# Odd rows of a finished chunk stored from ScalarE's transfer queue instead of SyncE's, in a two-layer convolution kernel

## What is computed

```python
# layer 0: depthwise 3x3, then three 64x64 channel mixes
dw  = conv(x, depthwise_weights, groups=64, padding=1)
att = einsum('cd,bdhw->bchw', softmax(attention_weights), dw)
pw  = einsum('kc,bchw->bkhw', pointwise_weights, att)
out = einsum('cd,bdhw->bchw', softmax(global_attention_weight), pw)
# layer 1: 3x3 convolution of signs with signed weights
xb  = sign(x);  bw = sign(clip(w, -1, 1)) * mean(abs(clip(w, -1, 1)))
out = conv(xb, bw, padding=1)
# both together; _gn is a group norm with 32 groups of 2 channels
x = x + layer0(_gn(x), ...)
x = x + layer1(_gn(x), w)
```

## Time and profile before

| | |
|---|---|
| median of three runs | 1862.25 us |
| the three runs | 1861.27, 1862.25, 1868.79 us |
| profiled execution, its own time | 1867.16 us |
| its span in the trace | 1865.3 us |
| mean granted TensorE clock | 0.998 |
| PE busy | 1767.8 us, 95% |
| DVE busy | 1603.3 us, 86% |
| ACT busy | 1333.6 us, 71% |
| POOL busy | 580.4 us, 31% |
| transfers | 271.39 MB, mean 145 GB/s |

### The profile page before, as it was taken

The page is one execution under the profiler, slowest core; times in us unless marked ns, Lnnn a source line. Parts: engine busy times, 40 slices in busy tenths (PEclk is TensorE's granted clock), DMA queues, the critical chain, the costliest instruction groups (busy, mean ns, idle before and its releaser), DMA issues.

```text
span 1865.3 us, 76406 instructions
## 1 busy us (share of the span) xinstructions
PE 1767.8 (95%) x33132; PEld 1535.2 (82%) x33132; DVE 1603.3 (86%) x2605; ACT 1333.6 (71%) x1460; POOL 580.4 (31%) x353
## 2 busy tenths in 40 slices
PE   0299999999999999999999999999999999999997
PEld 0299987799888887889988888779988888889996
DVE  5878889888998889888898888988899888877776
ACT  2277777677777776777777777777777777677774
POOL 1133333233233332333333333323333333333331
PEclk9999999999999999999999999999999999999999
DMA  9725665556555665656655666556655655433234
GB/s 283 194 81 159 158 152 143 153 153 154 148 150 163 154 153 143 158 149 155 158 138 160 159 156 154 142 159 153 153 146 155 164 151 153 103 82 75 74 77 103
DMA packets 278624, 271.39 MB, mean 145 GB/s; under 512 B 16112, under 2 KB 278320, under 8 KB 278464
## 3 DMA queue, kind: packets, MB, share of 16 engines
q1 hardware_dynamic: 269568, 260.11, 54.1%
q10 hardware_dynamic: 8448, 8.39, 1.6%
q0 software_dynamic: 448, 0.73, 0.2%
HBM read 134.95 MB, written 134.22 MB: 144 GB/s over the span
## 4 chain that ended last, share of the span: by engine, by line
PE 85%; DVE 8%; DMA 3%; issue 2%; ACT 2%; ACTq 0%; SPq 0%; DVEq 0%
PE psA L511 73%; PE psB L511 12%; DMA ring<-in_x 3%; DVE bnt L734 2%; DVE ring L944 1%; ACT xh L388 1%; DVE ring L910 1%; DVE psL L940 1%; DVE pk L921 1%; DVE aggr L848 1%; DVE xc L902 1%; ACT xn L384 0%; ACT xc L357 0%; DVE sums L750 0%; DVE ring L949 0%
## 5 line engine op out<-in xcount | busy, mean ns | idle before, releaser
L511 PE MATMUL psA<-xh,W 64*64 64x512 f16 x17912 | 1552.4, 373 | 15.6 <-DVE xh L969 6.6
L511 PEld LDWEIGHTS psA<-xh,W 64*64 64x64 f16 x17912 | 1080.9, 106 | 137.6 <-issue 71.3
L511 PE MATMUL psA<-xl,W 64*64 64x512 f16 x9216 | 989.9, 376 | 0.7 <-issue 0.6
L307 POOL TENSOR_TENSOR xl<-xc,xn 128x1024 f16<-128x1024 f32 (+1 forms) x320 | 570.8, 1794 | 1203.5 <-ACT xn L384 1187.9
L511 PEld LDWEIGHTS psA<-xl,W 64*64 64x64 f16 x9216 | 593.5, 107 | 38.1 <-issue 2.3
L511 PE MATMUL psB<-pk,W 64*64 64x512 f16 (+1 forms) x4944 | 604.9, 362 | 2.3 <-DVE pk L921 1.9
L388 ACT ACTIVATE xh<-xc 64x1024 f16<-64x1024 f32 (+2 forms) x622 | 574.5, 941 | 9.2
L384 ACT ACTIVATE xn<-xc 128x1024 f16<-128x1024 f32 (+2 forms) x262 | 270.8, 1036 | 278.1 <-PE psA L511 199.5
L910 DVE SCALAR_TENSOR_TENSOR ring<-psA,columns,ring 128x1024 f32<-128x1024 f32 x256 | 328.4, 1283 | 142.1 <-PE psA L511 141.9
L511 PEld LDWEIGHTS psB<-pk,W 64*64 64x64 f16 x4944 | 301.0, 106 | 64.8 <-issue 51.3
L734 DVE BATCH_NORM_STATS2 bnt<-ring 128x6 f32<-128x512 f32 x512 | 325.7, 681 | 30.7 <-DMA ring<-in_x 30.1
(11 more groups left out here) (104 smaller groups left out, 109.6 us busy)
## 6 DMA issues: line engine op xcount, KB each, us to landing
out_y<-ring SPq DMA_DIRECT2D x512, 256.0 KB, 3.3
ring<-in_x SPq DMA_DIRECT2D x448, 256.0 KB, 4.0
ring<-in_x SPq DMA_DIRECT2D x16, 512.0 KB, 16.8
ring<-in_x ACTq DMA_DIRECT2D x16, 512.0 KB, 16.5
pk<-in_w1T POOLq DMA_DIRECT2D x2, 144.0 KB, 7.2
ring<-in_w1n POOLq DMA_DIRECT2D x2, 144.0 KB, 8.0
grp<-in_same_group POOLq DMA_DIRECT2D x1, 64.0 KB, 7.3
ring<-in_dw POOLq DMA_DIRECT2D x2, 2.2 KB, 6.7
```

The source lines that it names most:

```text
L307: ins = nc.gpsimd.tensor_tensor(xl[:, slot:slot + rows, 1:W + 1], xc[:, j:j + rows], xn[:, k:k + rows, 1:W + 1], ALU.subtract)
L511: mm = pe.matmul(bank[out0:out0 + C, c0:c1], weights[src0:src0 + C, :], src[src0:src0 + C, slot:slot + rows, width[0]:width[0] + width[1]] ...
```

## The change

`store_chunk` on SyncE issues only the transfer of the even rows. A new `store_odd` on ScalarE issues the transfer of the odd rows of the same chunk, from ScalarE's own queue. In step t it stands behind the rounding of chunk t-3 and stores chunk t-4; in the tail it stands behind the signs, and then behind each of the last three roundings. It has the waits that the store on SyncE has: `y_rdy`, and the completion of the store of chunk g-2. The two transfers count up the same semaphore as before, so what the loads wait for is unchanged: both halves.

```diff
                 at = place(img, i)
-                for r in range(2):
-                    sp.dma_start(ov[img, r, :, i * G:i * G + G, :],
-                                 ring[64 * r:64 * r + 64, at:at + CE]).then_inc(stored[g % 2], 16)
+
+                sp.dma_start(ov[img, 0, :, i * G:i * G + G, :], ring[0:64, at:at + CE]).then_inc(stored[g % 2], 16)
...
+            def store_odd(g):
+                img, i = divmod(g, NC)
+                act.wait_ge(y_rdy, g + 1)
+                if g >= 2:
+
+                    act.wait_ge(stored[g % 2], 32 * (g // 2))
+                at = place(img, i)
+                nc.scalar.dma_start(ov[img, 1, :, i * G:i * G + G, :],
+                                    ring[64:128, at:at + CE]).then_inc(stored[g % 2], 16)
+
...
                 if t >= LAG:
                     round_of(t - LAG)
+                if t > LAG:
+                    store_odd(t - LAG - 1)
...
             for g in range(ALL + 1 - LAG, ALL):
                 signs_of(g)
+            store_odd(ALL - LAG - 1)
             for g in range(ALL - LAG, ALL):
                 round_of(g)
+                store_odd(g)
```

## The result

| | before | changed |
|---|---|---|
| median of 20 runs | 1866.47 us | 1869.14 us |
| lowest and highest | 1861.27, 1870.17 | 1866.87, 1870.94 |
| profiled execution (span) | 1867.16 (1865.3) | 1869.56 (1867.7) |

The ratio of the changed kernel to the one before is 1.0016, with a 95% interval from 1.0009 to 1.0023: 1.7 to 4.3 us slower. That is a real difference, though inside the 0.5% that the prediction called the same. Two of the three runs known at the time of the prediction (median 1862.25) were the two fastest of the 20; the median of all lies 4.2 us higher.

The account below looks back on a forecast made before the run. TensorE, busy 95%, was taken to bound the kernel. Steady part 0, loads 0 and tail +1.0 us gave 1868.2 us from the profiled execution, 1863.3 us moved to the median of the runs; range 1859.0 to 1870 us.

Parts of the forecast that it names:

- Steady part: ScalarE's steady steps: the new issue runs beside the rounding, its waits are already over, and `xn` is not delayed; 0 us.
- The 1.675 us: Longest issue of a store before the change, put behind the steady rounding as upper bound; still 0 on TensorE.
- the third rival: ScalarE's queue holds up issues in steady steps; beyond 2.3 us each tenth costs 26 us, 2.4 us gives 1889 us; chance 0.02.
- Loads: SyncE's loads behind the stores: in the typical step they go out at the same time as before; taken as 0 us.
- the room of 2.97 us: Steady step: time between a load's landing at 916.85 and VectorE's statistics at 919.82, more than the 2 us of possible lateness.
- The tail: Last three roundings delayed by issues ahead of them, less a saving at the last store: +1.0 us, ends -0.5 and +4.5.
- 0.3 + 0.62 + 0.62 = 1.54 us: Tail: delays of the last three roundings, each with a transfer issued ahead of it on ScalarE.
- The 0.52 us: End of the tail: saving from issuing the last store's two halves side by side, subtracted from the roundings' delays.
- saves 0.65, less what issuing at once costs: Last store: side-by-side issue saves 0.65 us, less 0.13 us because simultaneous issues take longer.
- The first: Steady loads: earlier loads remove VectorE's 13 waits; at most -6.7 us, giving 1856.6 us; chance 0.08.
- The second: Steady loads: stores land later and loads come late, deciding from about 3 us of added delay; 3.1 us gives 1884 us; chance 0.03.
- The fourth: Issues on the two queues exclude each other, so the odd half leaves as before; tail +1.5, 1863.8 us; chance 0.05.

Follow-up runs that it names:

- e4: Changed kernel with both halves of every store issued from ScalarE behind the rounding, also in the tail; SyncE only loads: ratio to before 0.9991, median 1864.68 us.
- e6: Changed kernel with the odd half of chunk t-5 stored behind the signs of step t, ahead of the rounding; tail order kept: ratio to before 0.9983, 1862.91 us.
- e10: Both halves of chunk t-5 issued from ScalarE behind the signs of step t, in the tail behind the roundings: ratio to before 1.0098, 1886.6 us.
- e5: Changed kernel with the odd half of chunk t-5 instead of t-4 stored behind the rounding of step t: ratio to before 1.3761, 2568.1 us.
- e1: Changed kernel with the last four chunks stored wholly by SyncE, as before the change: ratio to before 1.0005, median 1868.19 us.
- e3: Changed kernel with each odd store of the tail put behind the rounding, as in the steady part: ratio to before 1.0005.
- e7: The changed kernel again, the same program with an empty line: ratio to before 1.0018.
- e2: Kernel before with only the last four odd halves stored from ScalarE, each ahead of a rounding: ratio to before 1.0009.
- e9: Changed kernel with the odd half of chunk t-5 behind the signs of step t, in the tail behind the rounding: ratio to before 0.9964, 1860.27 us.

## Why the prediction was right, point by point

**Steady part, 0 us.** Right. The issue lies beside the rounding, the waits are over when it comes, `xn` starts when TensorE lets it. e4 shows that double the issues fit. The 1.675 us that I took as the bound of an issue and the 3.49 us of the third rival never came near: 0.652 us was the longest.

**Loads, 0 us.** Right within what the runs tell. Loads go out as early as before, and the room of 2.97 us is real: a delay of about 2.9 us (e6: issued at 907.74, where the rounding of the step before ran at 904.74) is borne, 3.6 us (e10) costs 1%, 6.8 us (e5) costs 700 us. VectorE's waits for loads were 11.5 to 14.4 us in the four profiles with the odd half behind the rounding (changed, e1, e3, e7) and 6.7 and 9.1 with the old store (before, e2). If that reaches the end at all, it is within the 1.0005 of e1 and e3, whose intervals hold 1.

**The tail, +1.0 us.** The place and the hold-up of the roundings were right, and this is the term that was mis-sized: 2.38 us in the first profile, 2.00 in e7's, 1.72 in e2's. The roundings were forecast 3.6 us apart and came 3.7 to 4.0 apart. Three parts of it:

- The three issues ahead of the roundings were put at 0.3 + 0.62 + 0.62 = 1.54 us. e2, the cleanest, has 0.40 + 0.68 + 0.68 = 1.76: each is 0.06 to 0.1 us more than forecast, since a rounding starts about 0.1 us after the end of the issue ahead of it.
- The 0.52 us to be saved by issuing the last two halves together did not come (0.01 us lost in the changed kernel, 0.05 saved in e2, both within the rounding of the spans). The step that failed is "saves 0.65, less what issuing at once costs". It priced the issue and forgot the data: the pair lands 3.89 us after its first issue whether the second issue follows at once or 0.44 or 0.64 us later. The two issues themselves took 0.60 and 0.64 us at the same moment, so they show no wait of a whole issue for the lock that the Trainium skill speaks of (Perfetto Trace Analysis, section "DMA Instruction — HWDGE (DVE, Sync)"); the data of the odd half began 2.55 us after its issue, that of the even half 1.25. The Trainium skill, page DMA: Bandwidth & Descriptors, section "Issuing engines are not separate DMA queues", says that transfers run on the same 16 transfer engines whichever engine issued them, so that issuing from several engines at once saves only sequencer time. The trace agrees: 0.64 us of sequencer time was saved and the landing went from 3.25 to 3.89 us. The same section has the transfers interleave; here their packets overlapped for only 0.25 us.
- 0.3 us of low clock in the first profile (not in e7's), and 0.3 us ahead of the third rounding in four of the profiles with one transfer ahead (changed, e5, e6, e7; not e2), unexplained.

**The time.** 1863.3 us against 1869.14 us. 4.2 us of the miss are the base, a median of three of which two were the fastest of 20; 1.6 us the tail and scatter. The medians of 20 lie 2.67 us apart, where +1.0 was forecast. The profiled execution, with 1868.2 as its sum, was nearer to the truth than the median of three. The range held the time, by 0.9 us, and that says little for the working: the range also holds the median of before, 1866.47 us. What bears the working out are the profiles and e1 to e4.

**Rivals.** The first (faster by earlier loads) and the third (ScalarE held up) found nothing. The second (loads too late) is real as a mechanism, as e5 and e10 show, and the change stays some 3 us short of it. The fourth, no gain in the tail from a second queue, came true by another cause, the data that goes out one half behind the other.

## What to carry to other kernels

A transfer that an engine issues is free where the engine's own program has the other engines wait for something else, and costs its issue time, here 0.68 us each, wherever another engine waits for the very next instruction; ask this of the first and last steps apart from the steady ones, and put the transfer behind the instruction that is waited for. Two queues shorten the issue, not the data. Where loads wait for stores through a full ring, work out how much later a store may go: up to that point its place in the step is free to choose, and here a better place was worth 0.36%.

## What was not expected of the hardware

In the tail TensorE's granted clock fell to 0.5 for 3.4 us behind an idle stretch of 1.9 us in two profiles (changed and e6), and kept 1.00 behind the same stretch while the work lasted in the ten others. In e5, where TensorE stood idle for `pk` 195 times (446.7 us), the mean granted clock of the whole run was 0.942, against 0.998 before; part of e5's time is that.

Separately, about 6 us of TensorE's idle time, up to 1.3 us at a time and with no releaser in the profile, went away when the odd half of the store moved 2.9 us later in the step: 0.3, 0.5 and 0.2 us in e6, e9 and e10, against 3.7 to 7.6 us in the eight profiles with both halves at the old place or beside the rounding. The trace says more about it than the table of waits. In these eleven profiles there are 70 such stretches of over 0.15 us behind the first 120 us, and every one of them ends 1.2 to 1.6 us after the end of a transfer on queue q8, which the page lists with the kind "instruction" (104 transfers, 1.70 MB). Such transfers start 5 to 8 us apart or further, so this is no chance: TensorE was very likely waiting for its own program. A transfer of that queue took 1.17 us before, 1.13 in e6 and 1.08 in e9 (medians). That the store's data holds up the program's when both move at the same time would fit, but no run tests it.
